# Moving three elementwise operations from VectorE to GpSimd in a gated linear-attention layer

## The reference

```python
x1 = layernorm(x)
r = sigmoid(x1 @ Wr.T);  k = x1 @ Wk.T;  v = x1 @ Wv.T
dec = sigmoid(decay)                       # one value per channel
scale = exp(t * log(clip(dec, 1e-7)))      # t = 0..4095
state = cumsum(k * v / clip(scale, 1e-10), axis=time) * scale
x = x + (rmsnorm(r * state) * ln_w) @ Wo.T
x = x + layernorm(x) @ (W + up_aux @ (lora_up @ (lora_down @ down_aux))).T + b
```

## Time and profile before

| | us |
|---|---|
| median of 3 runs (lowest, highest) | 937.92 (936.97, 938.16) |
| the profiled execution | 936.65 |
| its span, slowest core (the 8 cores: 931.8 to 935.1) | 935.1 |

### The profile page before, as it was taken

How to read it: one execution, slowest core, us unless ns; L and a number is a source line. 1 busy time by engine, 2 the same in 40 slices (tenths; PEclk the granted TensorE clock), 3 DMA queues, 4 the chain that set the end, 5 groups by cost and what they waited for, 6 DMA issues and landing times.

```text
span 935.1 us, 8679 instructions; the slowest of 8 cores (931.8 to 935.1 us)
## 1 busy us (share of the span) xinstructions
PE 544.5 (58%) x2558; PEld 251.9 (27%) x2558; DVE 359.4 (38%) x478; ACT 342.6 (37%) x458; POOL 77.7 (8%) x43
## 2 busy tenths in 40 slices
PE   1333313999586547667561714563456436799994
PEld 0223201433232213222220202221122112344442
DVE  2444400344343324344444043323331340566764
ACT  3665621443334434444544333231323221232332
POOL 1000000233121111111111001000000000000000
PEclk9999999999777959978886757766777577899998
DMA  4766402000101100000000110011001102233331
GB/s 145 217 203 204 134 7 66 1 0 1 43 25 46 44 25 23 22 22 23 23 23 0 38 44 32 23 45 46 22 22 46 46 0 67 68 136 136 135 128 75
DMA packets 19520, 56.27 MB, mean 60 GB/s; under 512 B 5934, under 2 KB 5934, under 8 KB 19474
## 3 DMA queue, kind: packets, MB, share of 16 engines
q1 hardware_dynamic: 19474, 55.73, 18.9%
HBM read 47.32 MB, written 8.39 MB: 60 GB/s over the span
## 4 chain that ended last, share of the span: by engine, by line
PE 29%; DVE 25%; ACT 21%; issue 10%; POOL 7%; DMA 4%; DVEq 1%; SPq 1%; ACTq 0%; POOLq 0%
PE psK L361 7%; PE psV L361 5%; PE psTb L263 4%; DVE u_m L470 4%; POOL k_m L464 4%; PE psV L589 4%; ACT lnT L349 3%; POOL k_m L402 3%; PE psR L635 3%; DVE yA L488 2%; ACT slotA L271 2%; ACT csbuf L460 2%; DVE u_m L382 2%; PE psTb L344 2%; DMA wstage<-up_aux 2%
## 5 line engine op out<-in xcount | busy, mean ns | idle before, releaser
L361 PE MATMUL psK<-lnT,slotA 128*128 128x512 bf16 x512 | 154.5, 469 | 2.0 <-ACT lnT L349 0.8
L361 PE MATMUL psV<-lnT,slotB 128*128 128x512 bf16 x512 | 115.7, 379 | 3.9 <-DVE u_m L382 3.9
L263 PE MATMUL psTb<-ident_t,castbuf 128*128 128x128 bf16 x224 | 28.3, 307 | 144.8 <-DVE castbuf L257 122.5
L361 PEld LDWEIGHTS psK<-lnT,slotA 128*128 128x128 bf16 x512 | 59.5, 117 | 88.6 <-issue 54.1
L361 PE MATMUL psR<-lnT,slotC 128*128 128x512 bf16 x256 | 64.4, 410 | 19.7 <-ACT csbuf L483 19.7
L464 POOL TENSOR_TENSOR k_m<-u_m,csbuf 128x1024 f32<-128x1024 f32 x16 | 37.4, 2340 | 386.9 <-ACT csbuf L460 386.9
L440 DVE TENSOR_TENSOR u_m<-k_m,psV 128x1024 f32<-128x1024 f32 x16 | 19.5, 1221 | 127.8 <-ACT csbuf L450 62.4
L361 PEld LDWEIGHTS psV<-lnT,slotB 128*128 128x128 bf16 x512 | 49.6, 98 | 65.7 <-issue 6.7
L263 PEld LDWEIGHTS psTb<-ident_t,castbuf 128*128 128x128 bf16 x224 | 21.7, 138 | 158.1 <-issue 158.1
L344 PE MATMUL psTb<-ident_t,yA 128*128 128x128 bf16 x192 | 23.1, 296 | 69.5 <-ACT lnT L349 47.4
L402 POOL TENSOR_TENSOR k_m<-u_m,csbuf 128x1024 f32<-128x1024 f32 x16 | 37.6, 2351 | 290.5 <-ACT csbuf L398 290.5
(11 more groups left out here) (128 smaller groups left out, 716.6 us busy)
## 6 DMA issues: line engine op xcount, KB each, us to landing
xt<-x_own SPq DMA_DIRECT2D x32, 512.0 KB, 3.8
xt<-x_pre SPq DMA_DIRECT2D x16, 512.0 KB, 6.7
wstage<-Wo SPq DMA_DIRECT2D x8, 512.0 KB, 3.3
xt<-Wf SPq DMA_DIRECT2D x8, 512.0 KB, 3.4
out<-k_m SPq DMA_DIRECT2D x6, 512.0 KB, 2.9
out<-u_m SPq DMA_DIRECT2D x5, 512.0 KB, 2.9
out<-csbuf SPq DMA_DIRECT2D x5, 512.0 KB, 2.9
wstage<-Wk SPq DMA_DIRECT2D x4, 512.0 KB, 4.4
```

The costliest lines, as they stand in the source:

```text
L263: return e.transpose(psTb[:, kc * 128:(kc + 1) * 128], cbuf[:, kc * 128:(kc + 1) * 128], ident_t[:])
L361: return e.matmul(ps[:, j * 512:(j + 1) * 512], wtile(slot, kc, m), lnT_mt(kc, h * H + j * 512, 512), start=(kc == 0), stop=(kc == 7))
```

## The change

Three operations of `mid_iter` are issued on POOL instead of DVE: the clip of the ramp (L456), the state product (L480) and the square (L494). Their operands and results stay as they are. The semaphores follow: ACT waits for POOL's count ahead of the exp and ahead of overwriting `rbuf`; `yA` (L488) waits for the tanh and for POOL's state product; the square waits for `yA`; the channel sums on PE wait for POOL's square. `trk["gpu"]` is now the count of the state product. The entry `y2_h`, which nothing read, is dropped.

```diff
--- before.py
+++ after.py
@@ -439,7 +439,7 @@
                                       ("gp", trk["gpu"][par])])
             def _(e, kB=kB, uB=uB): return e.tensor_mul(uB[:], kB[:], psV[:])
             trk["last_kv"] = c("ve")
-            @E("scalar", "sc", waits=[("ve", trk["state"][par])])
+            @E("scalar", "sc", waits=[("gp", trk["state"][par])])
             def _(e, m=m, h=h, rB=rB):
                 return e.activation(out=rB[:], in_=iota[:], func=AF.Exp,
                                     scale=small[:, 24 + m:25 + m],
@@ -451,11 +451,11 @@
                                     scale=small[:, 16 + m:17 + m],
                                     bias=bias_own[:, h * 8 + m:h * 8 + m + 1])
             sc_c2 = c("sc")
-            @E("vector", "ve", waits=[("sc", sc_c2), ("ve", c("ve"))])
+            @E("gpsimd", "gp", waits=[("sc", sc_c2), ("ve", c("ve"))])
             def _(e, kB=kB, cB=cB):
                 return e.tensor_scalar_min(kB[:], cB[:], 23.025850929940457)
-            ve_c = c("ve")
-            @E("scalar", "sc", waits=[("ve", ve_c)])
+            gp_c = c("gp")
+            @E("scalar", "sc", waits=[("gp", gp_c)])
             def _(e, kB=kB, cB=cB):
                 return e.activation(out=cB[:], in_=kB[:], func=AF.Exp)
             sc_ce = c("sc")
@@ -475,27 +475,26 @@
                 @E("vector", "ve", waits=[("ve", c("ve"))])
                 def _(e, m=m, uB=uB):
                     return e.tensor_copy(small[:, 48 + m:49 + m], uB[:, H - 1:H])
-            @E("vector", "ve", waits=[("gp", c("gp"))])
+            @E("gpsimd", "gp", waits=[("ve", ve_scan)])
             def _(e, kB=kB, uB=uB, rB=rB):
                 return e.tensor_mul(kB[:], uB[:], rB[:])
-            trk["state"][par] = c("ve")
+            trk["state"][par] = gp_state = c("gp")
+            trk["gpu"][par] = gp_state
             @E("scalar", "sc", waits=[("mm", mmr), ("ve", ve_scan)])
             def _(e, cB=cB): return e.activation(out=cB[:], in_=psR[:],
                                                  func=AF.Tanh, scale=0.5)
             trk["last_th"] = sc_r = c("sc")
-            @E("vector", "ve", waits=[("sc", sc_r)])
+            @E("vector", "ve", waits=[("sc", sc_r), ("gp", gp_state)])
             def _(e, m=m, h=h, kB=kB, cB=cB):
                 return e.scalar_tensor_tensor(yA_mt(m, h * H, H), cB[:],
                                               1.0, kB[:], ALU.add, ALU.mult)
             trk["yst"][par] = c("ve")
             y2w = [("mm", trk["mm_stats"])] if h == 1 else []
-            @E("vector", "ve", waits=y2w)
+            @E("gpsimd", "gp", waits=y2w + [("ve", trk["yst"][par])])
             def _(e, m=m, h=h):
                 return e.tensor_mul(y2A[:, m * H:(m + 1) * H],
                                     yA_mt(m, h * H, H), yA_mt(m, h * H, H))
-            trk["y2"] = c("ve")
-            if m == 7:
-                trk["y2_h" + str(h)] = c("ve")
+            trk["y2"] = c("gp")
 
         def mid_half_end(h, trk):
             ve_y2 = trk["y2"]
@@ -505,7 +504,7 @@
                 for mc in range(8):
                     w = []
                     if first:
-                        w = [("ve", ve_y2)]
+                        w = [("gp", ve_y2)]
                         if sc_evs:
                             w.append(("sc", sc_evs[-1]))
                         first = False
```

## The result

The changed kernel takes 975.77 us (median of 8 runs, 974.44 to 977.63) against 937.8 us before on the same chip (8 runs, 935.13 to 938.83). The ratio is 1.0409, 95% interval [1.0395, 1.0423]: 38 us slower. The forecast was 960, with a range up to 973.

What follows compares the result with a forecast made beforehand. One serial chain through `mid_iter`, with no engine near full, was taken as the bound. Half 0 -1.0 us and half 1 +4.6 give +3.4; blocking adds 18.7: 937.9 + 22.1 = 960.0 us, range 938 to 973.

Steps and rivals of the forecast that it cites:

- rival A: In half 1 the cast after `yA` is held behind POOL's square; 960 us, 953 to 968; chance 0.50.
- sign of being wrong: Forecast is wrong if half 0's iteration changes by over 0.5 us, or half 1's by less than 1 us.
- Part 1: Min before the exp moves to POOL, taking 1.2 us: +0.51 us per half 0 iteration, +0.45 in half 1.
- the clock: TensorE's granted clock in half 1's K product: six at 5.95 cost 1.5 us more, at 4.51 7.2 less.
- Part 4: After `yA`, POOL's square holds half 1's cast, +2.34 us in each of 8 iterations; half 0's statistics pay nothing.
- Parts 2 and 3: State product on POOL: +0.15 us under the tanh, +1.07 in seven half 1 iterations; square off DVE: -0.79, -0.87.
- The small copy L477: In half 0, if POOL's state product held this copy up, `yA` would be 0.32 us later 8 times, +2.6 us.
- Rival C: Min before the exp costs 2.34 us like a two-input operation, with no blocking: 959.5 us; chance 0.12.
- Rival D: Min at 2.34 us plus held cast, or half 0's statistics held too (18.7 more): about 979 us; chance 0.08.
- D's dear end: The costly end of the case put at about 979 us, left out of the range 938 to 973.

Runs made afterwards that it cites:

- the parts alone: Only the min, only the state product or only the square moved to POOL, each against the kernel before: 966.53, 939.35 and 932.21 us.

## Why the prediction was wrong

The direction was right, and so was the mechanism of rival A, the held cast. The price of the min was not, and it makes up more than half of the loss: +22.1 forecast, +38.0 measured. The prediction's own sign of being wrong came true as well: half 0's iteration grew by 1.41 us, where about -0.1 was forecast and 0.5 was the limit.

- **Part 1, the min: the step that failed.** It took 1.2 us for the operation, "half of two", with the two-input product's 2.34 as the upper end. The extra POOL instructions show that the product is no upper end: an operation with a constant takes 2.77 whatever it computes. Measured for the way to the exp: +2.11 and +1.99 instead of +0.51 and +0.45, 16 times some 1.57, 25 us. With 2.77 in place of 1.2 the forecast would have been 985, and the next two points and the clock bring that down to what was measured.
- **Part 4, the cast held by the square: the mechanism is shown, the price was too high.** Square 1.89 us and not 2.34, and the cast ends 0.55 after it instead of 0.79 (0.1 and its own 0.69). 1.65 us in place of 2.34 in each of 8 iterations, 5.5 us less. The statistics of half 0 stayed at 0.69 beside POOL, as assumed. The order of start came out as read from the handoffs, 0.14 against 0.23. By the Trainium skill (SBUF — State Buffer, "Who interferes with whom") the later of the two fully blocks; the runs agree for a square that reads and writes and for a fill that only writes.
- **Parts 2 and 3:** +0.15 and +1.07 forecast, +0.09 and +1.01 on the chain; -0.79, measured -0.80. Good to 0.1 us. The small copy L477, kept for the range, was not held: 0.15 us beside POOL's product.
- **The clock** was put at -7 to +1.5 us for one place, the K product. It gave about 2 us back there (on two of six cores, the slowest among them, it cost 1), and the parts alone show as much again behind half 1. The six later K products went neither to 4.51 nor to 5.95. A forecast from the chain alone is off by that much here, and so are sums of parts run alone.
- **Rival C** had the right place (before the exp, in both halves) but its price stopped at 2.34 and it excluded blocking. Rival D, "both", was the case that came, with 0.08. That its 979 was near is in part luck: the min at 2.77 instead of 2.34 adds 16 x 0.43 = 6.9 us, and the cheaper cast and the clock take about as much away. The range ended at 973 because it left out D's dear end, not only because of the min's upper end: with 2.34 for the min and the held cast the prediction's own terms give 978.
- Of the Trainium skill's rule that one-input operations on GpSimd run roughly at line rate (GPSIMD Engine Reference, "Engine selection"), the copy's 1.04 us agrees and the 2.77 us of min, product and sum with a constant don't: the measurement decides.

## What to carry to other kernels

An idle engine is no reason to move work to it when the work is a link of a serial chain: count the operation at the new engine's price, for its own form, and don't bound a form that was never timed by one with more inputs. Where two engines exclude each other, which one starts first decides who pays; release the operation nobody awaits from the end of the one that is awaited (here 12 to 14 us for one wait). And where a product on the path starts after idle time, its clock is a term of the sum.

## What was not expected of the hardware

- POOL, 1024 f32 columns: copy 1.04 us, two-input product 2.35, one tensor and a constant 2.77. The bf16 square with two bf16 operands is shorter, 1.89.
- A DVE operation with two tensors in SBUF is held as well, and holds in turn. In the kernel with the extra POOL instructions, `b_bcast` is added (L610, else 1.23 us) while POOL's product runs:

```profile
818.36 1.28 DVE L604 SCALAR_TENSOR_TENSOR k_m<-psV,colsB,x1t 128x1024 f32<-128x1024 f32 x1 [0.64 <-PE psV L589]
...
819.38 2.35 POOL L881 TENSOR_TENSOR csbuf<-iota,rbuf 128x1024 f32<-128x1024 f32 x1
...
819.89 2.92 DVE L610 TENSOR_TENSOR u_m<-k_m,b_bcast 128x1024 f32<-128x1024 f32 x1 [0.24 <-DVE k_m L604]
821.87 2.06 POOL L882 TENSOR_TENSOR csbuf<-iota,rbuf 128x512 f32<-128x512 f32 x1
```

The addition takes 2.92 us and ends at 822.81, 1.08 after the product's end at 821.73; POOL's next product, on 512 columns, then takes 2.06 instead of 1.26. The two POOL copies that started behind such an addition, at 812.91 and 829.92, took 1.74 and 1.23 instead of 1.04 and ended 0.89 after it both times.
- With 32 matmuls without use ahead of the first transposes and nine in each of the two gaps of 2.5 us the granted clock was at the 2.4 GHz level all through the K product; with the 32 alone it was not. The nine without the 32 were not run.
